# Where GpSimd clears the key buffer: behind the rotation tables, with two column clearings left out

## The reference

```python
x = x + attn_a(layernorm(x), ...)   # q = rope(rmsnorm(xh @ wq + bq)), k likewise; softmax; @ v; @ wo
x = x + ffn(layernorm(x), ...)      # router -> top 2 of 8 experts; silu(x Wg) * (x Wu) @ Wd
x = x + attn_b(layernorm(x), ...)   # linear attention over 4 memory banks, weighted by softmax(bank_weights)
x = x + ffn(layernorm(x), ...)
```

## Time and profile before

| | us |
|---|---|
| median of 3 runs (505.16 to 506.87) | 505.82 |
| the profiled execution | 503.61 |
| its span, from first to last instruction | 501.8 |
| TensorE busy in the span | 460.0 (92%) |
| VectorE busy | 362.8 (72%) |
| ScalarE busy | 266.6 (53%) |
| GpSimd busy | 251.0 (50%) |

### The profile page before, as it was taken

The page is one execution under the profiler, slowest core; times in us unless marked ns, Lnnn a source line. Parts: engine busy times, 40 slices in busy tenths (PEclk is TensorE's granted clock), DMA queues, the critical chain, the costliest instruction groups (busy, mean ns, idle before and its releaser), DMA issues. The chain is left out here.

```text
span 501.8 us, 11035 instructions
## 1 busy us (share of the span) xinstructions
PE 460.0 (92%) x3385; PEld 327.5 (65%) x3385; DVE 362.8 (72%) x1066; ACT 266.6 (53%) x642; POOL 251.0 (50%) x309
## 2 busy tenths in 40 slices
PE   6999999999999999999999879899979999999950
PEld 3546666777766677677777646585856876777740
DVE  6999999899899776853444648787798783444473
ACT  4579899988887775333333414734134342433310
POOL 6409569039742055574334556248475676333330
PEclk9999999999999999999999978999889999999985
DMA  5664710110420424464335393102124467233585
GB/s 173 254 248 175 179 34 13 59 29 12 135 68 34 114 76 140 133 205 129 106 106 179 66 193 56 43 12 93 57 95 132 137 190 213 81 106 108 193 298 169
DMA packets 43736, 60.78 MB, mean 121 GB/s; under 512 B 5856, under 2 KB 38240, under 8 KB 43040
## 3 DMA queue, kind: packets, MB, share of 16 engines
q1 hardware_dynamic: 33152, 37.72, 24.8%
q0 software_dynamic: 9984, 21.83, 14.4%
q10 hardware_dynamic: 544, 0.52, 0.3%
HBM read 28.89 MB, written 25.00 MB: 107 GB/s over the span
## 5 line engine op out<-in xcount | busy, mean ns | idle before, releaser
L1926 POOL DMA_INDIRECT ys<-yo,xin x78 | 76.2, 977 | 89.1 <-DVE yo L1746 78.9
L1179 PE MATMUL PS<-wexp,xTt 128*128 x312 | 106.0, 463 | 0.6 <-ACT xTt L1399 0.3
L1535 DVE TENSOR_REDUCE qa<-PS 128x1 f16<-128x512 f32 (+3 forms) x176 | 101.9, 637 | 5.5 <-PE PS L1051 4.9
L1361 ACT ACTIVATE prob<-PS 128x512 f16<-128x512 f32 (+1 forms) x176 | 92.2, 567 | 12.6 <-PE PS L1075 11.8
L1911 POOL DMA_INDIRECT xs<-xn,pos x64 | 62.6, 979 | 62.1 <-DVE pos L1620 46.0
L1199 PE MATMUL PS<-wexp,hT 88*128 x312 | 79.0, 382 | 2.5 <-ACT hT L1411 2.5
L1733 DVE SCALAR_TENSOR_TENSOR sg<-th,PS 128x176 f32<-128x176 f32 x78 | 26.2, 336 | 69.7 <-ACT th L1405 69.3
L1199 PEld LDWEIGHTS PS<-wexp,hT 88*128 88x128 f32 x312 | 57.0, 189 | 18.4 <-issue 4.0
L1179 PEld LDWEIGHTS PS<-wexp,xTt 128*128 128x128 f32 x312 | 53.6, 190 | 19.3 <-issue 1.8
L1073 PE MATMUL PS<-qT,kbd 128*128 128x512 f16 (+3 forms) x256 | 61.4, 299 | 0.8 <-ACT prob L1361 0.7
L1049 PE MATMUL PS<-kbd,qT 128*128 128x512 f16 (+1 forms) x176 | 59.1, 360 | 2.1 <-DVE qa L1535 1.5
(11 more groups left out here) (209 smaller groups left out, 822.7 us busy)
## 6 DMA issues: line engine op xcount, KB each, us to landing
xin<-xs SPq DMA_DIRECT2D x78, 129.0 KB, 2.3
wexp<-in_experts SPq DMA_DIRECT2D x4, 1216.0 KB, 9.8
kbd<-ys SPq DMA_DIRECT2D x18, 256.0 KB, 4.1
xs<-zeros SPq DMA_DIRECT2D x32, 129.0 KB
xn<-xn SPq DMA_DIRECT2D x8, 512.0 KB, 3.3
xall<-ys POOLq DMA_DIRECT2D x6, 512.0 KB, 6.2
out<-xall SPq DMA_DIRECT2D x8, 256.0 KB, 3.6
kbd<-kT SPq DMA_DIRECT2D x60, 32.0 KB, 1.8
```

Of the source, the lines that this page charges most:

```text
L1179: mm = pe.matmul(PS[:, bank, 0:2 * FI], xTt[:, j % NXT, kc * P:(kc + 1) * P], wexp[:, bass.ds(expert[f, j], 1), kc * 2 * FI:(kc + 1) * 2 * FI]
L1361: act.activation(prob[:, u % NPR, 0:nr * w], PS[:, bank, 0:nr * w], ACT.Exp, scale=ATT_SCALE)\
L1535: dve.tensor_reduce(qa[:, b % 2, i, REP * g + r0:REP * g + r0 + nr, HD], PS[:, bank, 0:nr * w].rearrange("p (r w) -> p r w", r=nr), AX.X, ...
L1926: pool.indirect_dma_start(ys[f], bass.IndirectOffsetOnAxis(xin[:, j % NXIN, D + 1:D + 2].bitcast(I32), axis=0), yo[:, j % NYO], None).then ...
```

## The change

GpSimd's step "presets" ends with the constants; the clearing of `kbd` and of the zeros becomes a step of its own, "blanks", that stands behind "constants" on GpSimd, and what waited for the clearing in the list waits for it. The clearing of the extra column of `qa` before the first two batches is left out, since VectorE's first clearing covers it; the transposes of these batches wait for the presets of both engines instead, and the later ones count two less. The table of nudges is replaced: most of its 190 or so numbers differ. The diff without the greater part of that table:

```diff
-NUDGE = {("add", 0): 84.9, ("apply", 0): 170.1, ("apply", 1): -5.8, ("bank_shift",): 127.1, ("bias",): -22.7,
-         ("clear", 1): -3.2, ("clear", 2): -1.6, ("clear", 3): 30.6, ("combT", 0): -21.1, ("combT", 2): 2.2,
...
+NUDGE = {("add", 0): 80.5, ("apply", 0): 107, ("apply", 1): -30.6, ("apply", 2): -87, ("bank_shift",): 178.9,
+         ("banks",): -2.8, ("bias",): 49.8, ("blanks",): 6.3, ("choose", 0): 10.6, ("choose", 1): -42.1,
...
+         ("shiftedT", 2): -135.9, ("shiftedT", 3): -159.8, ("sines", 0): 80.7, ("sines", 1): 81.7, ("sines", 2): 20.3,
...
@@ front
-    w.add(POOL, r(), 0.15, "clear", b, after=old + [(POOL, "presets"), (DVE, "presets")])
+    if b >= 2:
+        w.add(POOL, r(), 0.15, "clear", b, after=old + [(POOL, "presets"), (DVE, "presets")])
+    else:
+        r()
...
                     w.add(a, r(), 1.2 if a == ACTE else 0.88, "place_keys", after=[(PE, "keysT" if a == ACTE else "first_keysT", *[b] * (a == ACTE)),
-                                                            (POOL, "presets")])
+                                                            (POOL, "blanks")])
...
-                w.add(SP, r(), 2.4, "place_keys", b, g, after=[(ACTE, "keysT", b), (POOL, "presets")] + [(PE, "second", b - 1, g, NU - 1)] * (b > 0),
+                w.add(SP, r(), 2.4, "place_keys", b, g, after=[(ACTE, "keysT", b), (POOL, "blanks")] + [(PE, "second", b - 1, g, NU - 1)] * (b > 0),
...
-                w.add(PE, r(), 0.23 * len(groups), "queriesT", b, n, after=[(e, "queries", b, p), (POOL, "clear", b)],
+                w.add(PE, r(), 0.23 * len(groups), "queriesT", b, n, after=[(e, "queries", b, p), (POOL, "clear", b) if b >= 2 else (DVE, "presets")],
@@ plan_work
-    w.add(POOL, -999, 6.4, "presets")
+    w.add(POOL, -999, 2.7, "presets")
+    w.add(POOL, -450, 3.9, "blanks", behind=[(POOL, "constants")])
     w.add(POOL, -500, 1.2, "constants", after=[(DVE, "scales"), (POOL, "presets")])
-    w.add(POOL, unit(6), 1.7, "late", after=[(SP, "load_late"), (POOL, "constants")])
+    w.add(POOL, unit(6), 1.7, "late", after=[(SP, "load_late"), (POOL, "constants")], behind=[(POOL, "blanks")])
@@ tensor
                         pe.wait_ge(q_ready[n > 0], b + 1)
-                        pe.wait_ge(cleared, b + 1)
+                        if b >= 2:
+                            pe.wait_ge(cleared, b - 1)
+                        else:
+                            pe.wait_ge(presets, 2)
@@ gpsimd
                         pool.memset(vaug[:], 1.0).then_inc(presets, 1)
+                    elif kind == "blanks":
                         pool.memset(kbd[:].bitcast(U32), 0).then_inc(kbd_cleared, 1)
                         pool.memset(zeros[:, 0:ROW - 1], 0.0)
...
                     elif kind == "clear":
                         (b,) = a
-                        if b >= 2:
-                            made(pool, "shiftedT", b - 2, NG - 1)
-                        else:
-                            pool.wait_ge(presets, 2)
+                        made(pool, "shiftedT", b - 2, NG - 1)
                         pool.memset(qa[:, b % 2, :, :, HD:HD + 1], 0.0).then_inc(cleared, 1)
```

36 lines of the change are left out of this document (added).

## The result

| | before | after |
|---|---|---|
| median of 7 runs each, us | 506.09 (501.85 to 509.44) | 511.19 (509.66 to 511.98) |
| ratio, with its 95% interval | | 1.0107 (1.007 to 1.0144) |
| profiled execution, us | 503.61 | 511.8 |
| its span, us | 501.8 | 510.0 |

The changed kernel is slower by about 5 us. The forecast was 504.5 with a range of 501 to 509: wrong in sign, and outside the range.

The account below looks back on a forecast made before the run. It took TensorE as nearly full from 12.5 us to the tail and VectorE where attention begins, with no slack from 22 us. Start -0.3 and order -1.0 gave -1.3 us on the median 505.82: 504.5, range 501 to 509.

Parts of the forecast that it names:

- Parts 1 and 2: Start: clearing leaves GpSimd's front, projection 0.5 us earlier; clearing then runs 10.7 to 14.4, delaying the sines by 1.04.
- the -0.3 taken for the start: Net gain of the moved clearing at the start, in us, bounded between -0.9 and +1.1.
- Rival (b): Start: clearing holds VectorE's cosines, +0.5 to +1.1 us, order worth nothing; chance 0.14, shared with an order costing little.
- Part 3: Start: the two column clearings (0.65 us) go, and the query transposes that wait for the presets instead cost nothing.
- Rival (d): Start: sines come ahead of the clearing, which ends at 22.1, so the first key copy waits 2.4: 508.2 us; chance 0.04.
- Part 4: All stages: the new table of nudges changes the order, -1.0 us, won at the memory layer's seams, between -10.0 and +4.8.
- nothing there has slack: From 22 us to the tail nothing can absorb a shift, so a shift of the start passes through to the end.
- a shift that changes sharply at one stage: Sign that the nudges and not the clearing act, expected above all at 290 to 304 or 360 to 380 us.
- The price of a slow stretch: Memory layer's two seams: half clock at 300 to 304 and 368 to 370 us loses 2.0 and 1.0 us.
- Rival (c): Memory layer's end: one more VectorE step ahead of the scaling, a longer TensorE wait, 509.3 to 510.3 us; chance 0.19.

Follow-up runs that it names:

- move_alone: Kernel before with its order kept, only the clearing moved behind the tables and the two column clearings left out: 508.38 us, ratio 1.0030.
- order_alone: Changed kernel with its new order, but the clearing put back behind GpSimd's presets, in front of the tables: 510.20 us, ratio 1.0067 against the kernel before.
- the four filled kernels: Unused products in TensorE's waits: new order, start only, 510.52 us; start and 150 to 380 us: new order 505.84, old order with moved clearing 504.59, kernel before 503.44.
- the two filled kernels of the old order: Old order with unused products in TensorE's waits at the start and from 150 to 380 us: clearing moved 504.59 us, kernel before 503.44 us.
- the filled new order: Changed kernel with unused products added in TensorE's waits up to 27 us and from 150 to 380 us: 505.84 us, ratio 1.0015 against the kernel before.

## Why the prediction was wrong, point by point

- **Parts 1 and 2, the start: the steps right, some sizes off.** The held scalar step, the projection (10.11 for "about 10.1") and the place of the clearing came as worked out. GpSimd's cast of the bias took 0.56 instead of 0.84, so the tables ended at 10.45 and not "as before" at 10.74, and the six sine products took 4.05 instead of 5.02, ending at 18.17 for 19.4. On VectorE the sum of squares moved ahead of the rotation, as forecast; the 768 elements of cosines took 1.25 for 0.95 and the second scalar step 0.57, so the rotation started at 17.25 for 16.8 and the keys ended at 19.17, outside the 17.9 to 19.0 that were given and no earlier than before. That the constants land at 8.56 "in any case" holds for that one trace: in the eight traces of before, after, move_alone, order_alone and the four filled kernels GpSimd starts on them at 7.71 to 8.56. The gain hangs on it. Where the last queries end, the -0.3 taken for the start became -0.1 in after, -0.2 in move_alone, and -0.8 between the two filled kernels of the old order, where they landed at 7.78 and 7.71.
- **Rival (b), held cosines: no.** They lay at 12.82 to 13.58, beside the clearing that lasted to 13.90, and took 0.42 each, no more than the 0.43 of the earlier trace rows. The Trainium skill (SBUF — State Buffer, Who interferes with whom) says that an instruction of VectorE with two SBUF inputs contends only with a GpSimd instruction that reads SBUF. A clearing only writes, and the trace agrees. Beside the sines, which read, one of the two is held, and not always the same one. In the kernel before the second 256 elements took 0.65 beside a sine; the 768 took 0.95, and the sine that started with them took 1.72, where the two of its size took 0.91 and 0.92 in after. In after the 768 took 1.25, and the sine that started with them 0.43, beside 0.42 for the shortest of its size. The kernel before:

```profile
13.66 0.65 DVE L1497 TENSOR_TENSOR rota<-qk,rope 128x256 f32<-128x256 f16 x1
...
15.33 0.95 DVE L1497 TENSOR_TENSOR rota<-qk,rope 128x768 f32<-128x768 f16 x1
```
```profile
15.34 1.72 POOL L1832 TENSOR_TENSOR rotb<-qk,rope 128x384 f32<-128x384 f16 x1
```

- **Part 3: right.** No TensorE wait for the two columns shows up.
- **Rival (d), clearing behind the sines: no** (10.39 to 13.90, ahead of them).
- **Part 4, the order: this step failed.** I took -1.0 us, between -10.0 and +4.8, and the new order alone costs 3.4 us (1.6 to 5.2; 2.9 by the medians, of which an estimated 1.2 goes with the clock). The value had the wrong sign; the bound of +4.8 is not passed by order_alone, though the whole change comes to 5.1. It was taken from what there was to win at two seams of the memory layer, and the argument passed over attention, with the clause that nothing there has slack. But an order can lose there: attention's part of it is 3 us by 170 us in four traces of the new order against one of before. My reading of the windows is that TensorE and VectorE take turns as the bound, and that a trade in favour of the one at 60 to 75 us is paid by the other at 90 to 120; no run shows that by itself. The sign that the prediction named for the nudges, a shift that changes sharply at one stage, did come in the memory layer, but also in attention, where it looked for one shift from 60 to 260 us. And of the winnings nothing came: TensorE's wait for VectorE's scaling in the memory layer became 5.4 us in three pieces, where the earlier trace rows have 4.7.

```profile
PE PS L1244 <- DVE qa L1782: 5.4, 3, 2.5
...
PE PS L1229 <- DVE qT L1764: 2.3, 2, 2.1
```

- **The price of a slow stretch: mis-sized.** I took the two seams' stretches of the earlier trace rows for 2.0 and 1.0 us and as things that stay where they are. The window at 300 to 304 shows 4 us of a stretch that lasts from 295.0 to 305.2, half of whose busy time is 4.3 us. Nor do they stay: before has 17.0 us of them in one execution, move_alone 27.2 in the same order.
- **Rival (c), one more wait at the memory layer's end** gave 509.3 to 510.3, and the time is near. But its mechanism isn't what happened, so that the nearness is luck: the longest wait there became shorter (2.5 for 2.8), more than a third of the lag is there by 170 us, the old order of move_alone loses 5.2 us by 380 as well, and the filled new order loses nothing there.
- **The move's own cost stays open.** Two comparisons, move_alone and the two filled old orders, give it +0.30% and +0.25% (1.1 and 1.2 us by the medians), each barely or not beyond its uncertainty, while the traces show it 0.1 to 0.7 us ahead to 170 us. By the line the clocks account for 1.2 and 0.8 us of it. So if it is real, it goes with the clock further on; no run here shows why.

## What to carry over

A new order for the whole program isn't a side effect of a small edit: split the two, and run each alone, before any of the time is put down to the edit. Where two engines are both nearly full, "no slack" doesn't mean that the order can't matter: a new order with the same work lost 3 us there. Count the stretches at half clock, and compare many runs with many, before a trace's difference is called a cause. And where TensorE waits in a stage that alternates with VectorE, unused products in its waits were worth more here (0.5% to 0.8% on the kernel before, 1% on the kernel after) than the start that the change was about.

## What the runs showed of the hardware

The granted clock falls to 0.50 in stretches that lasted 3.4, 6.8 or 10.2 us ahead of the tail, and with the same sequence of TensorE's instructions they fall in other places from one execution to another (before and move_alone). The times of the kernel before spread over 2% (500.71 to 511.64) and go with the mean granted clock. One profiled execution is therefore not a baseline for a change of under 1%; its stretches at half clock have to be counted first.

A wait of 2.18 us that ended at 25.84 was followed by 3.4 us at half clock, and the kernel with filler in that wait had 1.00 there, but the same 3.4 us cost nothing that could be measured; VectorE had 3.40 of 3.40 us of work beside it with either clock. Not every such stretch follows one long wait: from 340 us to the one at 356.4 in the kernel before, TensorE's longest wait was 0.69 us.

A GpSimd clearing held a small scalar step of VectorE until the last clearing of a row was done: 2.52 us with the two columns in the row, 1.85 without them (order_alone), 0.17 with no clearing beside it.
